# AdaLN-FFN, two layers, one core: who splits the prepared expert weights, behind which instruction, and in how many raw buffers

## What is computed

```python
base1 = x @ W1.T + b1
for k in range(2):
    oh = one_hot(idx_topk[:, k], 8)
    z1 = (u1 * oh).reshape(N, 64)              # u1 = x through A1
    h = gelu(base1 + z1 @ B1_rf * 2.0)
    z2 = ((h through A2) * oh).reshape(N, 64)
    res += w_topk[:, k:k+1] * (h @ W2.T + b2 + z2 @ B2_rf * 2.0)
```

## Time and profile before

| | before |
|---|---|
| median of 3 executions | 1057.41 us (1055.34 to 1060.26) |
| the profiled execution's own time | 1054.48 us |
| its span | 1052.9 us |
| PE busy | 1009.4 us, 96% of the span, 4894 matmuls |
| VectorE busy | 597.3 us, 57% |
| GpSimd busy | 389.3 us, 37% |
| ScalarE busy | 260.5 us, 25% |
| DMA | 202.04 MB, mean 192 GB/s |
| the chain that ended last | PE 79%, VectorE 14%, DMA 2%, ScalarE 2% |

### The profile page before, as it was taken

The page is one execution under the profiler, slowest core; times in us unless marked ns, Lnnn a source line. Parts: engine busy times, 40 slices in busy tenths (PEclk is TensorE's granted clock), DMA queues, the critical chain, the costliest instruction groups (busy, mean ns, idle before and its releaser), DMA issues.

```text
span 1052.9 us, 14889 instructions
## 1 busy us (share of the span) xinstructions
PE 1009.4 (96%) x4894; PEld 834.4 (79%) x4895; DVE 597.3 (57%) x905; ACT 260.5 (25%) x433; POOL 389.3 (37%) x411
## 2 busy tenths in 40 slices
PE   8899999999999899899999999999999999999995
PEld 5678887778877688677776778777889999999994
DVE  3888778678596787857767442475362222222221
ACT  3743322111121112111233211120113333332221
POOL 4334433555654565545324100003113333333332
PEclk9999999999999999999999999999999999999998
DMA  7387545878868788697645210100664786786843
GB/s 237 133 301 275 173 153 171 291 240 295 296 219 298 242 292 297 219 344 247 244 138 198 82 40 1 40 1 1 222 250 77 234 240 174 249 238 166 247 72 40
DMA packets 65197, 202.04 MB, mean 192 GB/s; under 512 B 9812, under 2 KB 11108, under 8 KB 64644
## 3 DMA queue, kind: packets, MB, share of 16 engines
q1 hardware_dynamic: 41476, 124.21, 35.0%
q0 software_dynamic: 21488, 75.26, 23.9%
q10 hardware_dynamic: 2192, 2.08, 0.7%
HBM read 129.42 MB, written 72.10 MB: 191 GB/s over the span
## 4 chain that ended last, share of the span: by engine, by line
PE 79%; DVE 14%; DMA 2%; ACT 2%; issue 1%; ACTq 1%; PEldq 0%; POOLq 0%; PEld 0%; DVEq 0%
PE ps_y L1749 5%; PE ps_y L1751 4%; PE ps_y L1750 4%; PE ps_h L1707 4%; PE ps_h L1708 4%; PE ps_h L1709 4%; DVE g_lo L1236 3%; PE ps_y L2018 3%; PE ps_y L2022 3%; PE ps_y L2017 3%; PE ps_h L1997 2%; PE ps_y L1992 2%; PE ps_h L1993 2%; PE ps_y L1997 2%; PE ps_y L1993 2%; PE ps_h L1992 2%
## 5 line engine op out<-in xcount | busy, mean ns | idle before, releaser
L1749 PE MATMUL ps_y<-w_hi,g_hi 128*128 (+1 forms) x256 | 103.8, 405 | 18.3 <-DVE g_lo L1236 18.3
L818 POOL DMA_INDIRECT out_x<-yt,slot_tok x39 | 61.6, 1580 | 157.3 <-DMA out_x<-yt,slot_tok 110.6
L1596 DVE TENSOR_TENSOR rgt_lo<-ps_u,rgt_hi 128x384 fp32r<-128x384 f32 x39 | 21.7, 557 | 166.5 <-ACT rgt_hi L1052 166.5
L1228 DVE TENSOR_TENSOR h<-h,wb 128x512 f32<-128x512 f32 x64 | 51.6, 806 | 105.4 <-ACT h L939 103.6
L933 ACT ACTIVATE h<-ps_h,bias 128x512 f32<-128x512 f32 x64 | 44.0, 689 | 238.5 <-PE ps_h L1716 238.5
L1707 PE MATMUL ps_h<-xt_hi,w_hl 128*128 128x512 f32 x256 | 100.2, 391 | 1.3 <-ACT lg_t L882 0.7
L1750 PE MATMUL ps_y<-w_lo,g_hi 128*128 (+1 forms) x256 | 101.2, 395 | 0.0
L1751 PE MATMUL ps_y<-w_hi,g_lo 128*128 (+1 forms) x256 | 101.1, 395 | 0.0
L1709 PE MATMUL ps_h<-xt_hi,w_hl 128*128 128x512 f32 x256 | 100.3, 392 | 0.0
L1708 PE MATMUL ps_h<-xt_lo,w_hl 128*128 128x512 f32 x256 | 100.2, 391 | 0.0
L1241 DVE TENSOR_TENSOR g_lo<-h,g_hi 128x512 fp32r<-128x512 f32 x64 | 79.6, 1244 | 2.2
(11 more groups left out here) (323 smaller groups left out, 2472.9 us busy)
## 6 DMA issues: line engine op xcount, KB each, us to landing
w_hl<-w1s_d SPq DMA_DIRECT2D x49, 704.0 KB, 4.6
e_d<-pre_hi POOLq DMA_DIRECT2D x42, 384.0 KB, 4.4
w1s_d<-w_hl SPq DMA_DIRECT2D x16, 704.0 KB, 6.1
eg_hi<-e_d SPq DMA_DIRECT2D x7, 1408.0 KB
eg_lo<-e_d SPq DMA_DIRECT2D x7, 1408.0 KB
w_raw<-in_w1b SPq DMA_DIRECT2D x16, 608.0 KB, 5.3
pre_raw<-in_we POOLq DMA_DIRECT2D x21, 384.0 KB, 5.9
u1t<-in_we POOLq DMA_DIRECT2D x21, 384.0 KB, 5.6
```

The lines of the kernel that those rows point to most:

```text
L818: pool.indirect_dma_start(out=out, in_=yt[t % 4][:], in_offset=None, out_offset=bass.IndirectOffsetOnAxis(ap=slot_tok[:, t:t + 1], axis=0) ...
L1228: tt(h1[u][:], h1[u][:], wb[:, v, :], ALU.mult).then_inc(gch, 1)
L1749: mm(ps_y[:, j, :], g_hi[u][:, cols], sl(w2_hi), start=first, **kw)
```

## The change

The work of a unit is shared out anew:

- **The copy to pre_hi moves to ScalarE** (`high_unit` there), placed in program order behind `gelu_second` of tile 17 + k. It waits for the landing of unit k, from unit 2 on also for the store of pre_hi of k-2 and for the subtraction of k-2.
- **The subtraction stays on GpSimd**, but waits for `g1_done` >= 21 + k, which is the end of VectorE's last operation (L1241) of tile 18 + k. The loads' waits for `d_done` go, but for units 0 and 1.
- **Order on GpSimd** per unit k: subtraction of k, store of its low half, store of the high half of k+1, then the load of k+2 (while k < 8) and of k+3 (for 7 <= k < 39).
- **A third raw buffer**, the columns 768 to 1535 of u1t, is used from unit 10 on (`raw_of`: units 0 to 9 alternate between buffers 0 and 1, and unit 10 is the first in buffer 2; from unit 8 on the cycle is 0, 1, 2). Its first load waits for `z_ok` >= 6, VectorE's last reading of these columns. Each load waits for the store of the low half of the unit that had the buffer before.
- The final waits count three buffers, and GpSimd waits for the last stores at n == 1 of its `low_s` loop.

The amount of data, the number of DMAs and all arithmetic stay the same. The core of the diff:

```diff
+    IN_TWO = 8
+    raw_of = [k % 2 if k < IN_TWO else (k - IN_TWO) % 3 for k in range(AHEAD)]
+    raw_used = [raw_of[:k].count(raw_of[k]) for k in range(AHEAD)]
...
-        pre_raw = [sb_ahead("pre_raw0", [P, UW])[:], u1t[:, 0:UW]]
+        pre_raw = [sb_ahead("pre_raw0", [P, UW])[:], u1t[:, 0:UW], u1t[:, UW:2 * UW]]
...
             def load_unit(k):
-                u = k % 2
-                pool.wait_ge(d_done, 2 + FT + max(k - 1, 0))
-                if k >= 2:
-                    pool.wait_ge(pre_lo_st[u], 16 * (k // 2))
+                u = raw_of[k]
+                if k < 2:
+                    pool.wait_ge(d_done, 2 + FT)
+                if u == 2 and not raw_used[k]:
+                    pool.wait_ge(z_ok, 6)
+                if raw_used[k]:
+                    pool.wait_ge(pre_lo_st[u], 16 * raw_used[k])
                 at = k % UNITS * UW
                 pool.dma_start(pre_raw[u], we1[k // UNITS, :, at:at + UW]).then_inc(pre_in[u], 16)
 
-            def high_unit(k):
-                u = k % 2
-                pool.wait_ge(pre_in[u], 16 * (k // 2 + 1))
-                if k >= 2:
-                    pool.wait_ge(pre_hi_st[u], 16 * (k // 2))
-                nc.gpsimd.tensor_copy(pre_hi[u], pre_raw[u]).then_inc(pre_hi_done, 1)
+            def store_high(k):
                 pool.wait_ge(pre_hi_done, k + 1)
-                pool.dma_start(e_d[k // UNITS, 0, k % UNITS], pre_hi[u].bitcast(F32)).then_inc(pre_hi_st[u], 16)
+                pool.dma_start(e_d[k // UNITS, 0, k % UNITS], pre_hi[k % 2].bitcast(F32))\
+                    .then_inc(pre_hi_st[k % 2], 16)
 
             def low_unit(k):
-                raw = pre_raw[k % 2]
+                raw = pre_raw[raw_of[k]]
+                pool.wait_ge(g1_done, 2 + FT + 3 + k)
                 nc.gpsimd.tensor_tensor(raw.bitcast(F32R), raw, pre_hi[k % 2].bitcast(F32), ALU.subtract)\
                     .then_inc(pre_lo_done, 1)
+
+            def store_low(k):
                 pool.wait_ge(pre_lo_done, k + 1)
...
             def units(ks):
                 for k in ks:
-                    high_unit(k)
+                    low_unit(k)
+                    store_low(k)
                     if k + 1 < AHEAD:
-                        load_unit(k + 1)
-                    low_unit(k)
+                        store_high(k + 1)
+                    if k < IN_TWO:
+                        load_unit(k + 2)
+                    if IN_TWO - 1 <= k < AHEAD - 3:
+                        load_unit(k + 3)
 
             shared_at = (NS - 2) * FT + 2
             load_unit(0)
+            load_unit(1)
+            store_high(0)
             units(range(shared_at))
...
+            def high_unit(k):
+                act.wait_ge(pre_in[raw_of[k]], 16 * (raw_used[k] + 1))
+                if k >= 2:
+                    act.wait_ge(pre_hi_st[k % 2], 16 * (k // 2))
+                    act.wait_ge(pre_lo_done, k - 1)
+                nc.scalar.copy(pre_hi[k % 2], pre_raw[raw_of[k]]).then_inc(pre_hi_done, 1)
...
                     gelus(s * FT + f, f, f % 2, s - 1 if f == 1 else None)
+                    if 0 <= (s - 1) * FT + f - 1 < AHEAD:
+                        high_unit((s - 1) * FT + f - 1)
```

More of the change, by code:

```diff
@@ L347, in adaln_ffn @@
         out_st = sem("out_st")
-        pre_in = [sem(f"pre_in{u}") for u in range(2)]
+        pre_in = [sem(f"pre_in{u}") for u in range(3)]
         pre_hi_done = sem("pre_hi_done")
@@ L351, in adaln_ffn @@
         pre_hi_st = [sem(f"pre_hi_st{u}") for u in range(2)]
-        pre_lo_st = [sem(f"pre_lo_st{u}") for u in range(2)]
+        pre_lo_st = [sem(f"pre_lo_st{u}") for u in range(3)]
         half_in = sem("half_in")
@@ L643, in _ @@
                 sp.wait_ge(pre_hi_st[u], 16 * (AHEAD // 2))
-            for u in range(2):
-                sp.wait_ge(pre_lo_st[u], 16 * (AHEAD // 2))
+            for u in range(3):
+                sp.wait_ge(pre_lo_st[u], 16 * raw_of.count(u))
             sp.wait_ge(gu_done, NS * SH)
@@ L721, in low_unit @@
             def low_unit(k):
-                raw = pre_raw[k % 2]
+                raw = pre_raw[raw_of[k]]
+                pool.wait_ge(g1_done, 2 + FT + 3 + k)
                 nc.gpsimd.tensor_tensor(raw.bitcast(F32R), raw, pre_hi[k % 2].bitcast(F32), ALU.subtract)\
                     .then_inc(pre_lo_done, 1)
+            def store_low(k):
                 pool.wait_ge(pre_lo_done, k + 1)
-                pool.dma_start(e_d[k // UNITS, 1, k % UNITS], raw).then_inc(pre_lo_st[k % 2], 16)
+                pool.dma_start(e_d[k // UNITS, 1, k % UNITS], pre_raw[raw_of[k]]).then_inc(pre_lo_st[raw_of[k]], 16)
@@ L771, in _ @@
                     pool.wait_ge(a_done, STEPS)
+                    for u in range(3):
+                        pool.wait_ge(pre_lo_st[u], 16 * raw_of.count(u))
                 elif n == 3:
@@ L1261, in low_s @@
                         dve.wait_ge(pre_hi_st[u], 16 * (AHEAD // 2))
-                    for u in range(2):
-                        dve.wait_ge(pre_lo_st[u], 16 * (AHEAD // 2))
+                    for u in range(3):
+                        dve.wait_ge(pre_lo_st[u], 16 * raw_of.count(u))
                 hi, lo, raw = shared_halves(n)
```

## The result

| | kernel before | kernel after |
|---|---|---|
| median of 12 executions, same chip | 1056.41 us (1051.09 to 1062.08) | 1065.60 us (1060.31 to 1071.92) |
| the profiled execution: its own time, its span | 1054.48, 1052.9 us | 1060.31, 1058.7 us |
| ratio after to before | | 1.0099, 95% interval 1.0074 to 1.0125 |

The change made the kernel 1.0% slower; 1063 us was forecast.

What follows compares the result with a forecast made beforehand. PE was taken as the bound, busy 1009.4 of 1052.9 us. Terms -15.5 + 18.0 + 3 + 1 = +6.5 us took the median from 1057.4 to 1063.9, less 1 us for lighter traffic: 1063 us, range 1050 to 1077.

Steps and rivals of the forecast that it cites:

- The gain: Layer 0's units: subtractions moved out of VectorE's way save PE 15.5 us of its 18.8 us idle there.
- The four stalls: Two-buffer stage, loads 2 to 9: late units hold ScalarE's copy, gelu_first and PE, four times 4.5 us, 18.0 us lost.
- G: The end of tile 18+k on VectorE, from which the forecast timed the copy as due at G + 8.2 us.
- S + L - 5.2: Forecast stall in us per pair of units with two buffers; 4.5 us with the medians of S and L.
- S: Time from the issue of a unit's low-half store to its landing, median 4.0 us; L is the load's, 5.7 us.
- a balance: Rival: S + L between 7.5 and 9.4, stalls of 2.3 to 4.2 us, result about 1057 us; chance 0.3.
- The masks: Start of super tile 2: masks stand behind a 0.85 us copy on ScalarE, so PE loses 0.3 us.
- Three buffers: From unit 11: 2 stalls of 1.5 us in dense traffic, 3 us, plus 1 us for GpSimd delayed by slow stores.
- The clock: Rival: 1.2 GHz for half a step after each of four stalls, +15 us, 1079 us in all; chance 0.1.

Runs made afterwards that it cites:

- e8: Kernel after without the subtraction's wait for VectorE's tile; copy on ScalarE and third buffer kept: 1052.92 us, ratio 1.0007 to the kernel before.
- e7: Kernel before with only the copy moved to ScalarE, two raw buffers, no wait of the subtraction for VectorE: 1048.47 us, ratio 0.9919.
- e9: e7 with the third raw buffer from unit ten: 1044.34 us, ratio 0.9915 to the kernel before.
- e11: e9 with the subtraction's wait for the end of VectorE's tile 18+k added: 1079.91 us, ratio 1.0214 to the kernel before.
- e1: Kernel after with the masks made ahead of the unit's copy on ScalarE in tile f = 1: 1073.71 us, ratio 1.0157 to the kernel before.
- e12: e8 with the masks ahead of the copy on ScalarE: 1053.51 us, ratio 0.9968 to the kernel before.
- e3: Kernel after with two raw buffers for all 42 units, every load two units ahead: 1114.33 us in one run.
- e2: Kernel after with the copy of unit k moved between gelu_first and gelu_second of tile 18+k: 1066.67 us, ratio 1.0075 to the kernel before.
- e6: Kernel after with the copy placed as in e2 and every load issued two units ahead: 1062.68 us, ratio 1.0041 to the kernel before.
- e10: Kernel before with the third raw buffer from unit ten and nothing else: 1052.83 us, ratio 0.9986.
- e4: Kernel before with only the subtraction's wait for the end of VectorE's tile 18+k; copies stay on GpSimd: 1057.38 us, ratio 0.9996.
- e5: e4 with the third raw buffer from unit ten; copies stay on GpSimd: 1044.87 us, ratio 0.9878 to the kernel before.

## Why the prediction was right, and where its terms were not

The total, 1063 us (range 1050 to 1077), holds the measured 1065.60, and its direction is right. In its own terms it gave +6.5 us for the profiled execution; 5.8 were measured, of which 4.3 arose in layer 0. Term by term:

- **The gain, 15.5 us:** right. The low half's waits fell by 15.4 us; with `low_rank`'s 1.9 us, 17.3. The subtraction begins 0.1 us behind the tile for units 0 to 30, as estimated, and ScalarE's copies take 0.83 us (0.84 forecast).
- **The four stalls, 18.0 us:** right in place, number, chain and period, wrong in size: 9.5 us. In the second stall the subtraction began at 208.29 us, 0.1 us behind G, and the copy at 218.78: G + 10.6, against a due time of G + 8.2, so 2.4, with 2.18 measured. The formula S + L - 5.2 gives 2.8 to 3.4 us for the four, some 0.6 too much each, in part because a load went out 0.3 us behind the store's landing, not 0.6. The term that was mis-sized is S. The medians of before (4.0 and 5.7) were carried over; in the four chains the store landed in 2.7 to 2.9 us and the load in 5.3 to 5.7. That puts the stalls into the rival called a balance (2.3 to 4.2 us, about 1057 us). Why S is shorter is not shown. Thin traffic in the stalls is not the reason: the loads issued right behind the stalls (at 203.25, 221.09, 238.22 and 255.47 us) did land in 3.4 to 4.3 us, but no stall hangs on those, and the store of the second chain ran from 210.44 us, with a DMA share of 0.64 and 0.85 in the 8 us from 208 us. In before GpSimd's load, issued 2.7 us ahead of the low half's store, was still under way beside 41 of 42 such stores; beside the stores of the four chains no earlier transfer of GpSimd was. The stores between them had only the last 0.6 to 1.3 us of a load beside them and landed in 2.6 to 2.9 us too. That this overlap is what lengthens a store was not tried.
- **The masks, 0.3 us:** the step that failed. The prediction counted only the 0.85 us of the copy ahead of the masks. It missed that this copy itself waits for the subtraction of two units before, and this one for the end of VectorE's tile at a boundary: 4.4 us in one wait, 4.6 in both. e8, without that wait, has no such wait of PE.
- **Three buffers, 3 + 1 us:** in size about right (1.9 us for `gelu_first` at 464 us, 2.4 us for SyncE's load at 485 us), though the second is not a stall of a unit, as the prediction counted it. GpSimd's late subtractions came as told: units 31 to 36 begin 2.0 to 4.7 us behind their tile, and the four loads of shared weights, issued at 444.9 us in before, went out at 470.06 us and met SyncE's 1 MB load of acc (468.24 us); the DMA share was 1.01 to 1.04 from 474 to 486 us. That this meeting made SyncE's load late was read, not tried.
- **The clock, 0 us in the sum, a rival at 0.1:** partly come true, and elsewhere. The four stalls left PEclk at 1.00; three waits later cost 3.7 us. The Trainium skill, "TensorE: Matmul & The Clock Gate", section "HAM oscillation — how this bites in real kernels", says that DMA waits between bursts of matmuls bring the array back to half clock each time. The trace agrees for three waits, one of them directly for a DMA, and not for the four stalls.

So two errors, 8.5 us too much for the stalls and 8.0 too little for masks and clock (4.3 and 3.7), cancelled within a microsecond. The chain was read rightly; the number was right by luck, and so was the sign: with stalls of 9.5 us the prediction's own sum is -15.5 + 9.5 + 3 + 1 = -2.0 us, and only the masks and the clock, which it had at 0.3 and 0, make the change a loss.

What the experiments add is which edit costs. The table is the core of the case (ratio to before). In e7, e9 and e11, as in e1 and e12, the masks stand ahead of the copy; e3 has its loads in the order of after. e2 (1.0075) and e6 (1.0041), with the copy between the activations, are not in it.

| copy by | subtraction waits for VectorE | two buffers | third buffer, loads in the order of before | third buffer, loads a unit earlier, as in after |
|---|---|---|---|---|
| GpSimd | no | 1 | 0.9986 (e10) | |
| GpSimd | yes | 0.9996 (e4) | 0.9878 (e5) | |
| ScalarE | no | 0.9919 (e7) | 0.9915 (e9) | 1.0007 (e8), 0.9968 (e12, masks first) |
| ScalarE | yes | 1.05 (e3, one run) | 1.0214 (e11) | 1.0099 (after), 1.0157 (e1, masks first) |

Each half of the change is harmless or gains by itself; both together lose. The line with the wait alone, with the copy on ScalarE, costs 3.0% (e9 to e11), 1.9% (e12 to e1) and 0.9% (e8 to after); with the copy on GpSimd it costs nothing (before to e4) or gains 1.1% (e10 to e5). The wait puts some 7.4 us, a tile, into a buffer's round (in e9 the subtractions begin 7.4 us in the median ahead of the end of the tile for which e11 waits), and the copy on ScalarE makes the activations queue behind the end of that round. With the copy on GpSimd the longer round is free (e4, e5), with the early subtraction the copy is (e7, e9). Three versions beat both kernels clearly: e5, by 1.2%, and e7 and e9, by 0.8%.

Not tried: the loads of the shared weights at another time, what makes a store land in 2.7 or in 4.0 us, and whether e5 and e9 differ (they ran on different chips).

## What to carry to other kernels

When work moves to an engine that the bound depends on, write down everything that work waits for, each buffer it overwrites too, and hold the whole round (load, copy, subtract, store, load) against the step; a wait that cost nothing on an idle engine can be paid on the new one, beyond what that engine's own idle time covers. Aligning a collision away lengthens the round of the buffers in it, so an alignment wants either a spare buffer or a consumer that nobody queues behind. When halves of a change interact, run each alone: here the sum of the parts had the other sign.

## What the hardware showed that was not expected

- The length of a wait alone doesn't tell whether TensorE's clock falls. In after, 2.48 us at 203 us left it at 1.00; in e11 a wait of 2.47 us at 203 us, in nearly the same place, was followed by a stretch that ran in part at 1.2 GHz (14 matmuls where after has 20):

```profile
200.00:204.00 4.00, 1.53 (x4) 1.16 (x4) 0.00 (x0) 1.53 (x3) 1.54 (x3) 0.83 0.50 204
204.00:208.00 4.00, 4.00 (x14) 3.15 (x13) 3.25 (x6) 1.42 (x2) 0.00 (x0) 0.74 0.58 142
```

  (columns as in the table of stretches: PE, PEld, DVE, ACT, POOL, PEclk, DMA share, GB/s). Eleven waits in e11 cost 28.9 us, and PEclk is 0.96, 0.95 and 0.92 over its stretches from 160, 250 and 430 us. What tells the two cases apart stays open.
- ScalarE's copy took 818 to 842 ns in all 42 units of after, beside whatever VectorE and GpSimd did, while VectorE's g_lo takes 0.69 us alone and 2.58 us beside a subtraction. The Trainium skill, "SBUF — State Buffer", section "Who interferes with whom", says that VectorE and GpSimd share a pair of ports and that ScalarE waits for nobody; the trace agrees.
